# Attention on one core: TensorE makes a slot's transposes and next scores ahead of its projection, output and V products

## What is computed

```python
q = rope((xn @ q_w + q_b)...)        # 16 heads of 64
k = rope((xn @ k_w + k_b)...)
v = (xn @ v_w + v_b)...
scores = einsum('bhqd,bhkd->bhqk', q, k) * scale
attn = softmax(where(causal, scores, -inf))
ctx = einsum('bhqk,bhkd->bhqd', attn, v)
attn_out = ctx @ o_w + o_b + xn
```

## Time and profile before

| | |
|---|---|
| median of 3 runs | 2506.57 us (2506.34 to 2511.28) |
| the profiled execution's own time | 2507.55 us |
| its span, first to last instruction | 2505.6 us |
| what lies around the span | 1.95 us |
| one attention part, first batch | from 182 to 510 us |

### The profile page before, as it was taken

One profiled execution on the slowest core, in us unless ns is written; L12 is line 12 of the kernel. 1 busy time (PEld: TensorE's weight loads), 2 busy tenths in 40 slices (PEclk: granted clock), 3 DMA queues, 4 the chain that ended last, 5 costly groups with the idle time before them and its releaser, 6 DMA issues.

```text
span 2505.6 us, 41253 instructions
## 1 busy us (share of the span) xinstructions
PE 2063.1 (82%) x10326; PEld 1363.4 (54%) x10326; DVE 1666.8 (67%) x2947; ACT 1440.3 (57%) x2785; POOL 920.0 (37%) x797
## 2 busy tenths in 40 slices
PE   3749999879675999987966699996996669999698
PEld 1236666547324666655732466664662256666466
DVE  3957676669485666647948666674794766666488
ACT  2517676647542766655744366674674346766366
POOL 1544343223164434313315444341332453434222
PEclk9879999979796999997979799999897979999899
DMA  2000000001000000001100000000110000000011
GB/s 60 0 26 5 9 8 0 1 28 40 10 0 26 10 5 8 0 1 34 34 10 0 26 10 5 8 0 9 30 30 10 13 14 8 9 4 0 11 34 32
DMA packets 36210, 35.48 MB, mean 14 GB/s; under 512 B 3992, under 2 KB 30976, under 8 KB 36096
## 3 DMA queue, kind: packets, MB, share of 16 engines
q1 hardware_dynamic: 36096, 34.14, 4.7%
HBM read 32.03 MB, written 2.10 MB: 14 GB/s over the span
## 4 chain that ended last, share of the span: by engine, by line
PE 59%; DVE 20%; issue 10%; ACT 5%; POOL 4%; DVEq 1%; ACTq 0%; DMA 0%; POOLq 0%; SPq 0%
PE ps L1341 10%; PE ps L1180 7%; PE ps L1181 7%; PE ps L1182 7%; PE ps L1330 6%; DVE state L930 6%; PE ps L1320 4%; PE ps L1321 4%; PE ps L1356 3%; PE ps L1448 2%; PE ps L1208 2%; DVE q_split L993 2%; PE ps L1172 2%; DVE bx L923 2%; DVE ps L1008 1%
## 5 line engine op out<-in xcount | busy, mean ns | idle before, releaser
L707 ACT ACTIVATE probsT<-ps 128x512 f32<-128x512 f32 (+3 forms) x768 | 349.6, 493 | 382.4 <-PE ps L1330 381.7
L695 ACT ACTIVATE probs<-ps,least 128x640 f32<-128x640 f32 (+7 forms) x512 | 380.6, 743 | 65.4 <-DVE least L1003 59.5
L1330 PE MATMUL ps<-ident,probs 128*128 128x128 f32 x2304 | 349.4, 279 | 10.4 <-ACT probsT L707 10.2
L1320 PE MATMUL ps<-k_high,q_split 128*128 128x512 f32 (+3 forms) x768 | 309.2, 403 | 57.8 <-POOL k_low L550 38.6
L1330 PEld LDWEIGHTS ps<-ident,probs 128*128 128x128 f32 x2304 | 262.9, 141 | 128.2 <-issue 91.6
L538 POOL TENSOR_TENSOR roped<-turned 128x512 f32<-128x512 f32 x128 | 192.6, 1506 | 286.1 <-DVE turned L978 274.2
L1341 PE MATMUL ps<-probsT,vals 128*64 128x512 f32 (+3 forms) x1536 | 290.4, 502 | 5.2 <-ACT probsT L707 5.2
L1003 DVE CUSTOM_DVE_ANT_0 ps<-ps,row_masks 128x128 f32<-128x128 f32 (+3 forms) x256 | 127.6, 499 | 235.2 <-PE ps L1321 232.5
L1010 DVE TENSOR_REDUCE least<-ps 128x1 f32<-128x640 f32 (+3 forms) x256 | 262.3, 1025 | 9.1
L1321 PE MATMUL ps<-k_low,q_split 128*128 128x512 f32 (+3 forms) x768 | 259.0, 349 | 0.0
L755 ACT ACTIVATE hid<-ps,cols 128x512 f32<-128x512 f32 x256 | 176.4, 689 | 105.2 <-PE ps L1182 77.1
(11 more groups left out here) (213 smaller groups left out, 4252.2 us busy)
## 6 DMA issues: line engine op xcount, KB each, us to landing
w<-in_w SPq DMA_DIRECT2D x128, 128.0 KB, 2.0
w_pair<-in_w_pairs SPq DMA_DIRECT2D x36, 256.0 KB, 2.7
xin<-in_x SPq DMA_DIRECT2D x5, 512.0 KB, 3.9
out<-acc SPq DMA_DIRECT2D x4, 512.0 KB, 4.1
pos<-in_c_pos SPq DMA_DIRECT2D x1, 512.0 KB, 5.5
v_w<-in_v_w SPq DMA_DIRECT2D x1, 512.0 KB
o_w<-in_o_w SPq DMA_DIRECT2D x1, 512.0 KB
v_b<-in_v_b SPq DMA_DIRECT2D x1, 512.0 KB
```

Of the source, the lines that this page charges most:

```text
L695: act.activation(probs[:, t % 2, 0:width(t)], banks(2 * (t % 2))[:, 0:width(t)], ACT.Exp, bias=least[:, t:t + 1], scale=-1.0, accum_out=ro ...
L707: act.activation(dst, ps[:, T_BANK + g % 2, 0:k1 - k0], ACT.Copy).then_inc(t_taken, 1)
L1320: pe.matmul(o, q, k_high[par][h][:, k0:k1], start=True, stop=False)
L1330: made = pe.transpose(ps[:, T_BANK + g % 2, at - k0:at - k0 + P], probs[:, t % 2, at:at + P], ident[:, :])
```

## The change

In `step` of TensorE the transposes T(t - 1) and the scores S(t + 2) are moved ahead of all of X(t); in `step` of DVE least(t + 2) (with `invert` of slot 1 and the input norm) is moved ahead of the answers to X(t). ACT, POOL and the DMA queues are untouched. Since unit 9's scores are the first of the odd units to reach bank 3, one wait is put in slot 7 ahead of them: that the projection of slot 5 has been taken out of bank 3.

```diff
@@ DVE, step
                     for t in range(UNITS_A):
+                        if t == 1 and not first:
+                            invert(n - 1, 1)
+                        if last and t in NORM_AT:
+                            input_norm(NORM_AT.index(t), b + 1, root_at(b, R_NEXT), 3 * b + 2, 1)
+                        if t + 2 < UNITS_A:
+                            smallest(n, t + 2)
+                        elif not last:
+                            smallest(n + 1, t + 2 - UNITS_A)
                         if t < 8 and not last:
                             turned_of(n + 1, p + 1, at("proj", t), t, proj_bank(t))
...
                         if t in LOW_AT and not last:
                             low(n + 1, 1 - par, LOW_AT[t])
-                        if t == 1 and not first:
-                            invert(n - 1, 1)
                         if t == TILES + 1:
                             invert(n, 0)
-                        if last and t in NORM_AT:
-                            input_norm(NORM_AT.index(t), b + 1, root_at(b, R_NEXT), 3 * b + 2, 1)
-                        if t + 2 < UNITS_A:
-                            smallest(n, t + 2)
-                        elif not last:
-                            smallest(n + 1, t + 2 - UNITS_A)
@@ TensorE, step
                     for t in range(UNITS_A):
+                        if t > 0:
+                            turn_probs(n, t - 1)
+                        elif not first:
+                            turn_probs(n - 1, UNITS_A - 1)
+                        if t + 2 < UNITS_A:
+                            if t == 7 and not last:
+                                bank_free(at("proj", 6))
+                            scores(n, par, t + 2)
+                        elif not last:
+                            scores(n + 1, 1 - par, t + 2 - UNITS_A)
                         if t < 8 and not last:
...
                         if t in PV_NEW_AT:
                             weigh_values(n, par, 0, parts(TPH, PV_NEW_AT, t))
-                        if t > 0:
-                            turn_probs(n, t - 1)
-                        elif not first:
-                            turn_probs(n - 1, UNITS_A - 1)
                         if last and t == SUM_SLOT:
                             global_sums(b + 1, 1)
-                        if t + 2 < UNITS_A:
-                            scores(n, par, t + 2)
-                        elif not last:
-                            scores(n + 1, 1 - par, t + 2 - UNITS_A)
```

## The result

The changed kernel takes 2591.17 us in the median of 4 runs (2588.95 to 2591.43); beside it the kernel before took 2506.93. The ratio is 1.033, with a 95% interval of 1.0312 to 1.0348: 84 us slower. The profiled execution took 2588.95 us, with a span of 2587.0.

The account below looks back on a forecast made before the run. TensorE was taken to bound the attention (busy 37.92 of 39.90 us). Six middle steps of +1.85, a first of +0.5 and a last of +2.1 make 13.7 a batch, 55 in four: 2562, said as 2560; range 2505 to 2595.

Parts of the forecast that it names:

- the likeliest case: Whole kernel: slower, 2560 us, own range 2545 to 2575; chance 0.38.
- V wait: Slot 10: second V product waits for DVE to empty bank 7, 1.14 us by the row; forecast to go almost whole.
- the signs that the prediction named: Profile after: ACT's copies wait 1.5 to 2 us (slot 8), scores' wait for exponentials about 80, V products' wait under 5.
- I had 1.85: Middle step: net loss of 1.85 us, summed as 0.65 + 0.8 + 0.4.
- the +0.4 booked for slots 13 to 1: Slots 13 to 1: ctxT made after the minimum, output product stalls 0.9, replacing an old wait of 0.5; net +0.4.
- 0.65 + 0.8: Middle step: net losses of 0.65 us from slots 8 to 10 and 0.8 us from slot 12.
- No old factors, so +0.5: First step: the 1.55 us stall falls away and 1.29 of wait goes; net +0.5 us.
- not 2.1: Last step: no values to gain on, no next scores; loss of 2.1 us.
- ACT had slack (2475): Faster rival, decided at slot 8: ACT's waits cost nothing and the V wait goes, 32 us less; chance 0.12.
- No change (2507): Rival: new stalls at slots 8 and 12 (2.3) are paid by waits that go and earlier exponentials; chance 0.10.
- The half case: Rival, 2530: the stall at one of slots 8 and 12 stands, the other is absorbed, about 0.9 a step; chance 0.25.
- The worse case, 2595: Rival: V wait stays, or late ctxT stops T(14), exp(15) and S(1); over 1 us more every step; chance 0.15.

Follow-up runs that it names:

- Kernel 3: The changed kernel with ACT's two copies of the factors moved from slots 8 and 12 to behind the exponentials of slots 9 and 13: 2518.66 us.
- kernel 7: The kernel before with only the spread transposes of slots 8 and 12 moved behind that slot's scores: 2543.09 us, 1.0137 of before.
- kernel 8: The changed kernel with factor copies behind the exponentials of slots 9 and 13, ctxT ahead of unit 15's minimum, high parts one slot later: 2470.92 us.
- kernel 9: kernel 8 with DVE's copy of the first V product ahead of slot 9's scaling, and q's second low part in slot 10: 2431.68 us.
- Kernel 4: The changed kernel with DVE's scaling of this pair's ctxT (slot 13) put back ahead of the minimum of unit 15: 2550.60 us.
- Kernel 5: The changed kernel with ACT's high parts of q and k one slot later (slots 6, 7, 10, 11): 2558.66 us.
- Kernel 6: The changed kernel with the last step's small sums product ahead of the V products of slot 3 instead of behind them: 2590.78 us.

## Why the prediction was right, and where it was short

The time lay inside the range (2505 to 2595), 4 us under its upper end; the likeliest case was right in kind and 31 us low, and its own narrower range (2545 to 2575) was missed by 16. That the range held is in part luck: its upper end was set by a V wait that stays, which did not happen, and what filled the range up was other work, the first and last steps, that the sum had too small.

**Right, and shown:** that ACT's copies of the factors, which were not moved, are what the new order runs into. S(10) to S(11) was put at 3.28 us and took 3.41; from S(11) to S(12) 2.44 and 2.45; S(14) to S(15) 4.02 and 4.04. Kernel 3 takes that away alone and gains 72 us; kernel 7 puts it alone into the kernel before and loses 35. The V wait is gone, as forecast. The clock in the middle steps did not fall. Most of the signs that the prediction named are there, with three sizes off. ACT's copies wait 2.94 us in slot 8 and 4.15 in slot 12, not 1.5 to 2. The row of scores waiting for exponentials came to 55.5 us, not 80, since S(11) shows 0.44 us and S(15) 0.28 of its own and the rest of the stall is shown ahead of T(8) and T(12), as a wait for probsT. TensorE's busy time in a middle step rose by 1.1 us.

The Trainium skill, "Perfetto Trace Analysis", section Matmuls, has independent groups rotate through PSUM banks; the prediction read from it that the V wait would stay whole, because both products use one bank. In the changed kernel it did not stay. It came back at 1.19 us in kernel 8, once the stalls ahead of it were gone, and kernel 9 removed it with both products still in one bank.

**The middle step: near, by errors of both signs.** It lost 2.12 us, and I had 1.85. The stretch from S(15) to S(1) of the next step holds the same work of TensorE in both kernels, and ctxT is waited for in it. Its end before, and its end in the changed kernel:

```profile
337.43 0.33 PE L1320 MATMUL ps<-k_high,q_split 128*128 128x128 f32 x1 [0.38 <-ACT probs L695]
```

```profile
389.52 0.31 PE L1320 MATMUL ps<-k_high,q_split 128*128 128x128 f32 x1
```

It took 5.29 us before (332.14 to 337.43) and 5.28 after (384.24 to 389.52), and the other middle steps of the first batch give the same within 0.1. So the +0.4 booked for slots 13 to 1 was too much. The wait for ctxT did grow, to 1.12, but it replaced all the waits that stood there before, 0.33 for ctxT, 0.19 ahead of T(14) and 0.38 ahead of S(1); I had left the last two in ("I leave them so"). Kernel 4 shows the wait to be on the path all the same: without it the stretch takes 4.08 us (384.29 to 388.37), and 40 us by 32 steps is 1.25. It is a gain that the new order could have had, not a loss against the order of before.

The whole loss of a middle step thus lies between S(1) and S(15), where the sum had 0.65 + 0.8. To divide it I set gaps between scores against each other and allow for the X work that the change moves across their ends (an estimate from starts in the two traces): S(10) to S(12) lost 0.7, S(14) to S(15) 0.7, both near the forecast; S(12) to S(14) lost 0.4 and S(1) to S(10) 0.25, where I had nothing.

**Missed: the first step.** "No old factors, so +0.5" left out a queue. The projections' results reach POOL a slot later, and ACT's high parts of q and k, which are not moved either, wait for POOL behind them, 0.98 and 1.67 us in the first step. In the whole span ACT waits for POOL ahead of each of these two copies in 8 places instead of 4, so once more in each first step and in no middle step; that the V products in the odd slots of a middle step are what hides it is my reading. I named POOL's work for S(0) as the only user of that chain. The first steps lost 5 us or more each instead of 0.5. Kernel 5 takes back 4.0 of it in the first batch; of its 32 us in all, about 7 come from middle steps (24 by 0.28) and 3 to 4 from last steps.

**Missed: the last step.** It lost 3.7, not 2.1. In slot 3, S(5) waits 5.03 us for an exponential held up by the input norm, and the V products now lie behind that wait instead of ahead of it. They take 3.68 us instead of 1.94, and the granted clock is 0.50 there (busy time by stretch, the changed kernel):

```profile
485.20:490.30 5.10, 5.05 (x13) 1.78 (x14) 2.26 (x8) 0.94 (x3) 0.00 (x0) 0.50 0.00 0
```

Before, the same products ran at 1.00 ahead of a wait of 3.93. (0.50 is the lower level, 1.2 GHz, 1.00 the upper, 2.4 GHz.) But the kernel before paid for its wait too: the granted clock was 0.70 in the 5.6 us behind it (470.40 to 476.00), and the V products of slot 5 took 2.33 us there. From S(4) to S(8) the changed kernel needs 15.02 us (479.39 to 494.41) against 13.34 (463.65 to 476.99), so the longer wait and the lower clock together cost 1.7. The share of the clock is not constant: in kernel 4, behind a wait of 5.08, the same products took 2.96. Kernel 6 shows that the sums product is not what costs; moving these V products was not tried, so this part is read from the traces and not tested.

**The rivals.** That ACT had slack (2475) is out: all 64 copies wait, and S(11) starts only behind the copy, keep(7) and exp(9). No change (2507) is out by 84 us. The half case is out because both stalls stand, 3.41 us from S(10) to S(11) and 4.04 from S(14) to S(15). The worse case, 2595, put the V wait or a late ctxT in every step. The V wait went; ctxT is late in every step, but against the kernel before that cost nothing. So the case came within 4 us of the time for a reason that was not its own.

## What to carry to other kernels

When work is moved one place later on one engine, walk every engine that answers it, not only the two that the edit touches: here the order on ACT was written for the old places, and three small moves there and on DVE turned 84 us of loss into 37 us of gain, and with the V copy's place on DVE into 75. Price an unmoved consumer by the chain behind it (copy, keep, exponential), not by its own 0.6 us. Test a repair in both orders: the same move of ACT's copies was worth 72 us in one and nearly nothing in the other.

## What was not expected

Waits can cost more than their own length. DVE's order without TensorE's made a step of 40.2 us into one of 57.8. In that step (501.00 to 558.80) TensorE is busy 43.9 us and idle 13.9; in the step of the earlier trace rows it is busy 37.9 and idle 2.0. So 11.9 us are more idle time, and 6.0 are more time for nearly the same count of products (234 and 232). These go with a granted clock of 0.91 in a stage that had 1.00; the V products behind a wait of 2.58 took 2.08 us instead of 1.16.
